# Moving two PE units of an attention kernel from steps 4 and 5 to steps 8 and 9

## What is computed

```python
h = group_norm(x, gn_w, gn_b)                  # 8 groups of 16 channels
q, k, v = qw @ h + qb, kw @ h + kb, vw @ h + vb
attn = softmax(q.T @ k / sqrt(128), axis=-1)   # 1024 x 1024
out = x + pw @ (v @ attn.T) + pb
```

## Time and profile before

| | us |
|---|---|
| median of 3 runs (lowest, highest) | 140.19 (140.17, 140.63) |
| profiled execution, whole | 140.34 |
| its span in the profile | 138.4 |
| PE busy in the span | 129.9 (94%) |
| DVE busy | 99.5 (72%) |
| ACT busy | 64.9 (47%) |
| POOL busy | 26.1 (19%) |

### The profile page before, as it was taken

The page is one execution under the profiler, slowest core; times in us unless marked ns, Lnnn a source line. Parts: engine busy times, 40 slices in busy tenths (PEclk is TensorE's granted clock), DMA queues, the critical chain, the costliest instruction groups (busy, mean ns, idle before and its releaser), DMA issues.

```text
span 138.4 us, 2200 instructions
## 1 busy us (share of the span) xinstructions
PE 129.9 (94%) x743; PEld 112.5 (81%) x743; DVE 99.5 (72%) x172; ACT 64.9 (47%) x112; POOL 26.1 (19%) x33
## 2 busy tenths in 40 slices
PE   5999999997878999999999999999999999999990
PEld 5986888885656888999898888899988889998880
DVE  0577788989999678979687789756987798330222
ACT  4044689655556574634347735354544334412000
POOL 5053050750202033300032063000030012003000
PEclk9999999999999999999999999999999999999999
DMA  4960000002998699569781998699825998997512
GB/s 133 279 271 0 0 5 0 10 31 63 203 211 200 166 208 206 154 149 211 158 219 47 207 207 179 206 203 209 199 97 122 207 207 222 216 216 169 167 38 76
DMA packets 9566, 21.00 MB, mean 152 GB/s; under 512 B 2362, under 2 KB 4052, under 8 KB 9556
## 3 DMA queue, kind: packets, MB, share of 16 engines
q1 hardware_dynamic: 8816, 20.59, 61.2%
q10 hardware_dynamic: 740, 0.28, 0.7%
HBM read 4.07 MB, written 2.11 MB: 45 GB/s over the span
## 4 chain that ended last, share of the span: by engine, by line
PE 87%; DVE 8%; issue 3%; POOL 0%; DVEq 0%; POOLq 0%
PE ACC L375 36%; PE S L322 10%; PE S L323 9%; PE S L326 9%; PE S L266 5%; PE A L302 5%; DVE s_sb L654 3%; PE S L350 2%; PE ACC L350 2%; DVE blocks L663 2%; PE ACC L402 1%; PE A L402 1%; DVE g_lo L628 1%; DVE bn L579 1%; PE A L278 1%
## 5 line engine op out<-in xcount | busy, mean ns | idle before, releaser
L375 PE MATMUL ACC<-pT,v 128*128 128x128 f32 (+1 forms) x320 | 53.3, 317 | 0.0
L654 DVE TENSOR_SCALAR_CACHE_REDUCE s_sb<-S,row_term 128x1024 f32<-128x1024 f32 x32 | 41.0, 1281 | 16.4 <-PE S L326 16.0
L375 PEld LDWEIGHTS ACC<-pT,v 128*128 128x128 f32 x320 | 46.4, 191 | 3.9
L500 ACT ACTIVATE s_sb<-s_sb,rowmin 128x1024 f32<-128x1024 f32 x32 | 36.9, 1152 | 20.9 <-DVE s_sb L654 19.8
L663 DVE STREAM_TRANSPOSE blocks<-s_sb 128x1024 f32<-128x1024 f32 x28 | 34.7, 1239 | 0.0
L322 PE MATMUL S<-h_hi,g_hi 128*128 128x512 f32 x64 | 29.2, 457 | 0.3 <-issue 0.3
L323 PE MATMUL S<-h_lo,g_hi 128*128 128x512 f32 x64 | 25.1, 393 | 0.0
L326 PE MATMUL S<-h_hi,g_lo 128*128 128x512 f32 x64 | 19.9, 392 | 0.0
L808 POOL TENSOR_TENSOR xb<-rden_bc,xb 128x512 f32<-128x512 f32 (+1 forms) x7 | 8.4, 1198 | 49.8 <-DVE rden_bc L683 42.3
L326 PEld LDWEIGHTS S<-h_hi,g_lo 128*128 128x128 f32 x64 | 12.0, 188 | 2.8
L322 PEld LDWEIGHTS S<-h_hi,g_hi 128*128 128x128 f32 x64 | 12.1, 189 | 2.2 <-issue 0.4
(11 more groups left out here) (90 smaller groups left out, 102.9 us busy)
## 6 DMA issues: line engine op xcount, KB each, us to landing
pT<-blocks SPq DMA_DIRECT2D x112, 128.0 KB, 2.5
rden_bc<-row_store SPq DMA_DIRECT2D x6, 256.0 KB, 3.4
x_sb<-x SPq DMA_DIRECT2D x1, 1024.0 KB, 6.3
out<-xb SPq DMA_DIRECT2D x8, 128.0 KB, 2.8
out<-xb SPq DMA_DIRECT2D x4, 256.0 KB, 2.9
x_sb<-x SPq DMA_DIRECT2D x2, 256.0 KB, 3.0
x_sb<-x SPq DMA_DIRECT2D x1, 512.0 KB, 4.1
w_in<-weights ACTq DMA_DIRECT2D x2, 128.0 KB, 3.5
```

Of the source, the lines that this page charges most:

```text
L375: last = pe.matmul(to, v[:, b % 3, t, :], probs[:, :, t, :], start=(t == 0), stop=(t == KT - 1))
L500: act.activation(s_sb[:, c % 3, :], s_sb[:, c % 3, :], ACT.Exp, bias=rowmin[:, c % CH:c % CH + 1], scale=-1.0, accum_out=den[:, n % 2, k:k ...
L654: dve.tensor_scalar(s_sb[:, c % 3, :], S[:, c % 2, :], row_term[:, b % 2, i:i + 1], None, ALU.add, ALU.min, accum_out=rowmin[:, i:i + 1]). ...
```

## The change

The two numbers that say at which steps the units of the first pair run become 8 and 9.

```diff
-FIRST_UNIT_STEPS = (4, 5)
+FIRST_UNIT_STEPS = (8, 9)
```

## The result

The changed kernel takes 147.40 us (median of four executions, 147.29 to 148.17), the kernel before took 140.36 on the same chip (140.17 to 140.63). The ratio is 1.051 with a 95% interval of 1.047 to 1.055: slower by 7.0 us, where 145.2 was forecast, with 144.3 to 147.8 as its range. The profiled execution took 147.29 us, its span is 145.3, against 140.34 and 138.4 before: 6.9 us more.

What follows compares the result with a forecast made beforehand. DVE was taken to bound steps 7 to 9 and PE everything from step 10. The units' new place (0.5 us) plus a PE stall behind the late store (4.5 us) gave 5.0 us: 145.2 us, range 144.3 to 147.8.

Steps and rivals of the forecast that it cites:

- What bounds the kernel: DVE sets the pace in steps 7 to 9, PE from step 10; PE delays after 43 us are paid in full.
- Part 1: Two PE units leave steps 4 and 5 for 8 and 9; gaps hold most of their 3.1 us: +0.5 us.
- DVE's lead at chunk 8: Without the early units and step 8's division, DVE's drain of chunk 8 starts about 1.0 us earlier.
- Part 2: SP's store of set 0 waits for POOL's late residual, moves of set 2 9.5 us late: 4.5 us PE stall, step 14.
- Part 3: Behind the stall: nothing added for later waits, SP caught up by set 4, none of the 5.0 us won back.
- DVE's wait at chunk 14: DVE's transpose waits 0.4 us, or 1.4, for set 2's moves; put at nothing, up to 0.8 in the range.
- The likeliest case: Stall of PE at step 14 with its clock kept: 145.2 us, chance 0.57.
- the first rival: PE's clock falls in the step 14 stall, adding 1.9 us: 147.1 us, chance 0.30.
- The two rivals in which the store holds nothing back: SP's waiting store doesn't delay set 2's moves: 140.7 us, chance 0.05; or DVE's lead also survives: 139.2 us, 0.03.
- the second stall: SP stays late and set 3's moves hold up unit 10 as well: 147.2 us, chance 0.05.
- The faster rival: Units fit PE's idle time in steps 8 and 9, DVE's 1.0 us lead survives to step 10: 139.2 us, chance 0.03.

Runs made afterwards that it cites:

- e7: e1 with 9 matmuls of the identity, read by nobody, put on the PE in its step 7 pause; 140.91 us, ratio 1.0035.
- e10: The kernel of e1 run once more for a trace; one execution, 141.39 us.
- e3: Changed kernel with 19 matmuls of the identity, read by nobody, put on the PE ahead of unit 6 to fill the stall; 146.62 us, ratio 1.0433.
- e4: Changed kernel with POOL's residual of set 0 ahead of the subtraction in step 12 instead of behind it; 142.40 us, ratio 1.0129.
- e9: Changed kernel with division and residual of set 0 at step 11 instead of 12, store in its old place; 141.15 us, ratio 1.0032.
- e1: Changed kernel with SP's store of set 0 behind the 16 moves of set 2 instead of ahead of them; 141.11 us, ratio 1.0047.
- e5: Kernel before with the units at steps 5 and 6, division and residual of set 0 at step 9; 139.67 us, ratio 0.9943.
- e8: e2 with SP's store of set 0 behind the moves of set 2; 140.17 us, ratio 0.9977.
- e2: Kernel before, units still at steps 4 and 5, with only division and residual of set 0 moved from step 8 to 12; 146.86 us, ratio 1.0434.
- e6: e5 with division and residual of set 0 at step 11 and SP's store of set 0 behind set 2's moves; 139.34 us, ratio 0.9922.

## Why the prediction was right, point by point

**What bounds the kernel.** Right. PE had no idle time behind step 10 but the one stall, and both the stall and the slow stretch were paid in full.

**Part 1, +0.5 us.** About right, and small for the reason given: DVE's lead was used up by units that came back ahead of scores that DVE waited for. The drain of chunk 8 was early, unit 0 ran from 36.70, and the scores of chunk 9 started at 38.33, those of chunk 11 at 45.92 instead of 45.03, 0.9 us late. 0.5 of these were there already at the scores of chunk 4 (22.46 against 21.95) and have nothing to do with the change; they come from a longer slow stretch at the start of that execution (last section). So the part itself was 0.4 us in the trace. Reckoned in the same way it was 0.4 us in e7 and e10 too, without the fall of step 7, and 0.6 to 0.9 us in e3, e4 and e9, with it; e1's ratio, over executions of both kinds, gives 0.7 us (0.4 to 0.9). DVE's lead at chunk 8, put at 1.0 us, was 1.26 us (e5). The pause of 1.9 us that the units leave behind in step 7 was not in the working, which had only said that DVE becomes the limit there.

**Part 2, the store.** Right in its place, its chain and nearly in its size: the moves started at 54.98 (forecast 54.75), the unit at 61.94 (61.7), the stall was 4.1 us (4.5). It was shorter because PE came 0.4 us later than worked out, by the slow start; the total doesn't feel that, since unit 6 waits for the moves and not for PE. e1 and e8 take the stall away, e2 makes it without the units, e4 scales it to 0.83 us (0.9 expected), and e9 shows that below the slack nothing is lost.

**Part 3.** Nothing for DVE's wait at chunk 14: right for the changed kernel, but only because the fall of the clock delayed the scores of chunk 15. With the stall filled (e3), and so without that fall, the wait was 1.31 us and cost 1.1, above the 0.8 left for it. So the nearest run to the forecast's own case, a stall with the clock kept, measured 146.6 us (e3) and not 145.2. Most of that gap is this term, put at nothing, though the slower issue of the moves in e3's trace has a share in it. SP had caught up at set 4, as worked out.

**The rivals.** The likeliest case had the clock kept, at 145.2 us; what came was the first rival, given 0.30, at 147.1. The range held both; the step of the forecast that failed is the weight between the two. The price was right, 1.69 us for unit 6 against 1.7 to 2.0 from the kernel's start. I had held the missing precedent in the trace against it; the kernel's start, where matmuls took 0.223 instead of 0.128 us after a pause of 1.57 us, was the nearest thing to one and should have weighed more. That 147.1 came so close to 147.40 is in part luck: DVE's wait of part 3, left out of it, was covered by the slow unit. The Trainium skill (TensorE: Matmul & The Clock Gate, "Why this matters for your kernels") warned of idle gaps between bursts, and the trace after agrees: 0.50 behind the pause of 4.1 us. The two rivals in which the store holds nothing back are out by SP's 12.0 us wait, with the moves behind it only at 54.98; the second stall is out too, since PE has no idle time behind unit 6.

The faster rival's condition, units that fit into PE's idle time without delaying scores, was real but at another place: steps 5 and 6 (e5, e6), where it gave 0.8 to 1.1 us.

## What to carry to other kernels

- When a piece of work moves, follow its last consumer on every in-order queue: what stands behind that consumer is moved too. Here a store that nobody needs early stood ahead of moves that everybody needs, and 9.7 us of delay less 4.5 us of slack were paid (5.2), with 1.7 us for the clock on top.
- Price a new stall of PE together with what its clock does behind it, and check whether a short fix (here one line of SP's program) removes both.
- Idle time of PE is worth something only where the inserted work doesn't delay what the bounding engine waits for next: the same 3.1 us cost 0.7 us ahead of chunks 9 and 10 and gained 0.8 us ahead of chunks 6 and 7.

## What the runs showed of the hardware beyond that

Shorter pauses than the stall can take the clock down as well. In e4 a pause of 1.89 us and one of 0.46 us, with PE busy for a few matmuls between them, were followed by a granted clock of 0.50 for about 3.5 us, and the same happened in the profiled executions of e3 and e9; the same pauses in the profiled execution of the changed kernel (1.89 and 0.46 us) and in e10 were followed by 1.00. So at such a length it differs from execution to execution, while behind 4.1 and 4.2 us it fell in both profiled executions that had them.

The start of the kernel differs too. The timeline of PE in the changed kernel, against the earlier trace rows:

```profile
6.07 0.78 PE L266 MATMUL S<-ident 128*128 128x128 f32 x2
...
9.41 1.28 PE L266 MATMUL S<-ident 128*128 128x128 f32 x10
```

The ten matmuls that began at 8.65 in the profiled execution of before begin at 9.41 here, since the slow pace lasted past 6 us (0.78 us for two that take 0.47 at full pace), with identical programs up to that point and a granted clock printed as 1.00. Differences of half a microsecond between two profiled executions of this kernel are therefore no evidence on a change.
